# Feed-forward up and gate projections by one level of Strassen's scheme, in a Mamba-2 layer with a ternary feed-forward

## The chip, the cores and the metric

One Trainium2 chip, one core of it. The metric is the device time of one launch in microseconds (us). It is given as the median of several runs; one more execution was taken by the hardware profiler, and its trace is what the rows below come from.

## The reference, cut to what matters

There are 2 sequences of 2048 tokens with 512 features. A Mamba-2 block (input projection, short convolution, state-space scan, gate, RMS norm, output projection) is followed by residual and layer norm, then by a gated feed-forward with ternary weights and again residual and layer norm:

```python
def ternary_quant(w):
    scale = jnp.mean(jnp.abs(w)) + EPS
    q = jnp.clip(jnp.round(w / scale), -1.0, 1.0) * scale
    return w + jax.lax.stop_gradient(q - w)
wu, wg, wd = ternary_quant(W_up), ternary_quant(W_gate), ternary_quant(W_down)
# x: [tokens, 512]; W_up, W_gate: [2048, 512]; W_down: [512, 2048]
# feed-forward: (silu(x @ wg.T or x @ wu.T) * the other one) @ wd.T
```

The kernel takes the silu of the "up" product and multiplies it by the "gate" product. The 4096 tokens make NB = 8 blocks of T = 512 tokens.

## The kernel before, in words

The kernel has two stages, one after the other, each with one program for every engine; semaphores tie the programs together.

**Stage A** (to about 813 us) does the Mamba-2 block and the first layer norm, block by block. Each block has four places p = 0 to 3, and the order within a place is written out by hand for each engine. Beside it the stage makes the ternary weights: in the places of blocks 2 to 5 a piece of W_up or W_gate, in those of blocks 6 and 7 a piece of W_down. A piece is loaded (`load_quant`, line 437), its signs are taken on ACT (line 827), `quantise` on DVE (line 1205) makes -1, 0 or 1 in float16, and `store_quant` (line 442) writes it to a DRAM scratch. When the last input projection is done, the weights of up and gate are loaded over the input projection's weights (`weights`, 2 x 2 MB, line 516). The layer norm's result goes to DRAM as `x1_dram`. In each place POOL gates two heads (`yg`, line 958), and scales and subtracts for others; it waits for DVE's `y_ch` first.

**Stage B** (from about 814 us) does the feed-forward. For a block n:

- `turn(n, k)`: PE transposes the block's float32 rows into PSUM, four pieces of 128 features. ACT writes the high float16 half `x_hi` (line 1503), DVE the low half `x_lo` (line 1545).
- `up_gate(n, par, m)` for m = 0 to 15: 8 matmuls (4 pieces of the features, each with `x_hi` and `x_lo`) of 128x128 weights and 512 columns for up, 8 more for gate (line 1460). They have two PSUM banks each for up and gate.
- `hidden(n, m)`: ACT takes tanh of up (line 1508), DVE makes (tanh + 1) * up (line 1551) and multiplies by gate (line 1556), ACT makes `h_hi` (line 1512), DVE `h_lo` (line 1561).
- `down(t, par, c)` for four groups c of 128 tokens: 32 matmuls of 512 columns (line 1474) into one of two banks; then DVE's residual, statistics, POOL's power -0.5 and DVE's `normalise`, and a store.

A step t does up and gate of block t+1, and the down product of block t: after every fourth m one `turn` of block t+2 and one `down`. Ahead of step 0 the up and gate of block 0 run with no down product between them; step 7 has down products only. The queue of each engine is in this written order, and an engine whose next instruction waits holds all that is behind it. POOL has nothing in stage B but one tiny power for each group of 128 tokens.

Of the kernel before, what the change touches and what calls it, by code (L numbers as in the profile page):

```python
# [24 lines left out]
F32 = mybir.dt.float32  # L25
# [5 lines left out]
P = 128  # L31
# [9 lines left out]
KF = 16  # L41
COL_CB = 2 * H * P
# [3 lines left out]
QW = FW // NB // 2  # L46
SU = 16.0
# [95 lines left out]
def build(nc, a, out):  # L143
    with ExitStack() as ctx:
        keep = {
            "cum_dram": nc.dram_tensor("cum_dram", [2, C, H, P], F32, kind="Internal").ap(),
            "tern_dram": nc.dram_tensor("tern_dram", [3, NB, P, 2 * QW], F16, kind="Internal").ap(),
# [10 lines left out]


            "x1_out": [ctx.enter_context(nc.semaphore(f"x1_out{k}")) for k in range(2)],  # L160
            "xin_in": ctx.enter_context(nc.semaphore("xin_in")),
            "tern_in": [ctx.enter_context(nc.semaphore(f"tern_in{w}")) for w in range(3)],
# [7 lines left out]
def stage_a(nc, a, keep):  # L170
    cum_dram, tern_dram, x1_dram = keep["cum_dram"], keep["tern_dram"], keep["x1_dram"]
    weights, ident, ffn_scale, exponent = keep["weights"], keep["ident"], keep["ffn_scale"], keep["exponent"]
    passed = keep["passed"]
    with ExitStack() as ctx:
# [35 lines left out]
        quant = sb("quant", [P, 2, 2 * QW])  # L210
        raw_q = quant[:, 0, :]
        sgn = quant[:, 1, 0:QW].bitcast(F16)
        tern = quant[:, 1, QW:2 * QW].bitcast(F16)
# [5 lines left out]
        u_hi = sb("u_hi", [P, 2, KD * T], F16)  # L219
        u_lo = sb("u_lo", [P, 2, KD * T], F16)  # L220
# [11 lines left out]
        cum_b = sb("cum_b", [P, 4, C, P])  # L232
# [55 lines left out]
        tern_ok = sem("tern_ok")  # L288

# [98 lines left out]
        def _(sp):  # L388
# [11 lines left out]
            def load_abs(i):  # L400
                if i >= N_ABS:
                    return
                if i >= 2:
                    sp.wait_ge(abs_ok[i % 2], i // 2)
                sp.dma_start(quant[:, i % 2, :], a["w_ffn"][i // NB, i % NB]).then_inc(abs_in[i % 2], 16)
# [29 lines left out]
            def load_quant(n, par, p):  # L435
                w, row = quant_row(n, par, p)
                sp.dma_start(raw_q, a["w_ffn"][w, row]).then_inc(rawq_in, 16)

            def store_quant(n, par, p):
                w, row = quant_row(n, par, p)  # L440
                wait_apart(sp, tern_ok, n * 4 + (p + 1 - 4 * Q0), passed["sp"])
                sp.dma_start(tern_dram[w, row], tern).then_inc(tern_out, 16)
# [13 lines left out]
            def step(n, par):  # L456
                for p in range(4):
# [11 lines left out]
                    if is_at(n, NB):  # L469
                        if p == 1:  # L470
# [36 lines left out]
                    if quantised(n):  # L507
                        store_quant(n, par, p)
                    if p == 3 and more(n):
                        store_cum(n + 1, 1 - par, turn_use(n, "cumt"))  # L510
                        load_cum(n + 1, 1 - par, 0)
                    if p == 3 and is_at(n, NB - 1):
                        sp.wait_ge(z_full, NB * H)
                        sp.wait_ge(tern_out, 16 + 16 * NB * 2)
                        for w in range(2):
                            sp.dma_start(weights[:, w * FW:(w + 1) * FW].rearrange("p (n q) -> p n q", n=NB),
                                         tern_dram[w].rearrange("n p q -> p n q")).then_inc(keep["tern_in"][w], 16)
# [209 lines left out]
        def _(act):  # L727
# [12 lines left out]
            def magnitude(i):  # L740
                act.wait_ge(abs_in[i % 2], 16 * (i // 2 + 1))
                act.activation(quant[:, i % 2, :], quant[:, i % 2, :], ACT.Abs,
# [80 lines left out]
            def signs(n, par, p):  # L823

                w, _ = quant_row(n, par, p)
                act.wait_ge(rawq_in, n * 64 + (16 * (p + 1) - 64 * Q0))
# [88 lines left out]
        def _(pool):  # L915
# [71 lines left out]

            def step(n, par):
                for p in range(4):
# [24 lines left out]
        def _(dve):  # L1014
# [14 lines left out]
            def magnitude(i):  # L1029
                dve.wait_ge(abs_in[i % 2], 16 * (i // 2 + 1))  # L1030
                dve.tensor_reduce(abs_sum[:, i // NB, i % NB:i % NB + 1], quant[:, i % 2, :], AX.X, ALU.add,
                                  apply_absolute_value=True).then_inc(abs_ok[1], 1)
# [290 lines left out]

def stage_b(nc, keep, out):
    tern_dram, x1_dram = keep["tern_dram"], keep["x1_dram"]
    weights, ident, ffn_scale, exponent = keep["weights"], keep["ident"], keep["ffn_scale"], keep["exponent"]
    passed = keep["passed"]
    with ExitStack() as ctx:  # L1328
# [9 lines left out]
        t_ug_k = weights[:, 0:2 * FW].rearrange("p (w k e) -> p w k e", w=2, k=KD)  # L1338
# [5 lines left out]
        x_hi = sb("x_hi", [P, 2, KD, T], F16)  # L1344
        x_lo = sb("x_lo", [P, 2, KD, T], F16)
        x_res = sb("x_res", [P, 2, D])
        th = sb("ffn_th", [P, 2, T])
        act_up = sb("act_up", [P, 2, T])
        hid = sb("hid", [P, 2, T])
        h_hi = sb("h_hi", [P, 2, KF, T], F16)  # L1350
        h_lo = sb("h_lo", [P, 2, KF, T], F16)
        res = sb("ffn_res", [P, 2, D])
        stats = sb("ffn_stats", [P, 2, 6])
        mv = sb("ffn_mv", [P, 2, 2])
        var_e = sb("ffn_var_e", [P, 2])
        rstd = sb("ffn_rstd", [P, 2])
        y = sb("ffn_y", [P, 2, D])

        p_up, p_gate, p_down, p_x = ([bank(f"p_{x}{k}") for k in range(2)] for x in ("up", "gate", "down", "x"))

        tern_in, xin_in = keep["tern_in"], keep["xin_in"]
        xres_in = [sem(f"xres_in{k}") for k in range(2)]
        y_out = [sem(f"y_out{k}") for k in range(2)]
        scales_ok = sem("scales_ok")
        px_full = sem("px_full")
        xhi_ok = sem("xhi_ok")
        xlo_ok = sem("xlo_ok")
        up_full = sem("up_full")
        gate_full = sem("gate_full")
# [12 lines left out]

        def run_steps(eng, step):

            step(0, 0)
# [10 lines left out]

        def has_turn(t):

            return not (is_at(t, NB - 1) or is_at(t, NB - 2))

# [3 lines left out]
        def _(sp):  # L1404
# [258 lines left out]
```

## Time and profile before

| | us |
|---|---|
| runs | 1514.17, 1510.38, 1513.2 (median 1513.2) |
| profiled execution, whole | 1507.89 |
| its span, first to last instruction | 1506.2 |
| PE busy | 1420.2 (94%) |
| DVE busy | 958.5 (64%) |
| ACT busy | 665.1 (44%) |
| POOL busy | 354.1 (24%) |

The page's own slices of the span (40 equal ones, each digit the busy tenths of a slice):

```
PE   5787999999999999999967999999999999999998
DVE  6696787887878778787643555555555545555453
ACT  4586385673746747476441333222222223222220
POOL 0044254462534525355350000000000000000000
PEclk9798999999999999999978999999999999999999
```

The stages are seen in the POOL row: it is at work in the first half and idle in the second. PE is full in both, except at the start and where the stages meet.

### The profile page before, as it was taken

The page shows a single profiled execution, that of the slowest core. Times are in us where ns is not written, and L with a number is a line of the kernel's source. Part 1 is how long each engine was busy: PE and PEld are TensorE (multiplying, and loading weights), DVE is VectorE, ACT ScalarE, POOL GpSimd, SP SyncE. Part 2 cuts the span into 40 slices and gives each one's busy share as a digit, 9 for nine tenths or more (in the row PEclk, how much of TensorE's full clock was granted, in tenths as well). Part 3 has the DMA queues.
Part 4 walks back from the last instruction along what each step waited for, and adds up shares of the span by engine and source line. Part 5 has one row for each costly group of instructions (what it writes and reads, how often), then busy time and mean ns, then how long its engine had stood idle before and what let it go on. Part 6 is the DMA issues. An engine that isn't in the chain of part 4 may idle for free. (4 is left out here: it accounts for less than half of the span.)

```text
span 1506.2 us, 22488 instructions
## 1 busy us (share of the span) xinstructions
PE 1420.2 (94%) x7978; PEld 736.3 (49%) x7978; DVE 958.5 (64%) x1697; ACT 665.1 (44%) x1344; POOL 354.1 (24%) x392
## 2 busy tenths in 40 slices
PE   5787999999999999999967999999999999999998
PEld 2354555555655555555543444444444444444443
DVE  6696787887878778787643555555555545555453
ACT  4586385673746747476441333222222223222220
POOL 0044254462534525355350000000000000000000
PEclk9798999999999999999978999999999999999999
DMA  4735334242242522316233010100201010100101
GB/s 144 236 116 177 105 88 133 72 148 72 81 138 71 148 82 86 130 62 167 86 133 122 5 42 28 57 25 11 64 21 64 14 57 29 56 24 12 35 22 63
DMA packets 93311, 121.48 MB, mean 81 GB/s; under 512 B 6672, under 2 KB 57616, under 8 KB 91920
## 3 DMA queue, kind: packets, MB, share of 16 engines
q1 hardware_dynamic: 93200, 120.01, 25.4%
q8 instruction: 68, 1.11, 0.3%
q14 instruction: 43, 0.35, 0.1%
HBM read 96.79 MB, written 23.20 MB: 80 GB/s over the span
## 5 line engine op out<-in xcount | busy, mean ns | idle before, releaser
L574 PE MATMUL ring<-u_hi,weights 128*128 128x512 f16 x1088 | 353.9, 387 | 5.1 <-DVE x_ch L1056 5.1
L574 PE MATMUL ring<-u_lo,weights 128*128 128x512 f16 x544 | 210.3, 387 | 0.0
L1460 PE MATMUL p_up<-x_hi,weights 128*128 128x512 f16 x512 | 195.1, 381 | 3.8 <-DVE x_lo L1545 3.8
L1460 PE MATMUL p_up<-x_lo,weights 128*128 128x512 f16 x512 | 195.1, 381 | 0.0
L1460 PE MATMUL p_gate<-x_hi,weights 128*128 128x512 f16 x512 | 194.8, 381 | 0.0
L1460 PE MATMUL p_gate<-x_lo,weights 128*128 128x512 f16 x512 | 194.6, 380 | 0.0
L1474 PE MATMUL p_down<-t_down,h_hi 128*128 128x512 f16 x512 | 194.1, 379 | 0.0
L1474 PE MATMUL p_down<-t_down,h_lo 128*128 128x512 f16 x512 | 194.1, 379 | 0.0
L1512 ACT ACTIVATE h_hi<-hid 128x512 f16<-128x512 f32 x128 | 80.7, 631 | 244.1 <-DVE hid L1556 244.1
L1508 ACT ACTIVATE ffn_th<-p_up,tanh_scale 128x512 f32<-128x512 f32 x128 | 88.0, 687 | 222.6 <-PE p_up L1460 222.5
L1536 POOL TENSOR_TENSOR ffn_rstd<-ffn_var_e,exponent 128x1 f32<-128x1 f32 x32 | 17.3, 540 | 673.3 <-DVE ffn_var_e L1573 673.3
L574 PEld LDWEIGHTS ring<-u_hi,weights 128*128 128x128 f16 x1088 | 108.9, 100 | 129.6 <-issue 12.4
L601 PE MATMUL ring<-w_out,raw 128*128 128x512 f16 x768 | 169.3, 381 | 0.0
L1551 DVE SCALAR_TENSOR_TENSOR act_up<-ffn_th,p_up 128x512 f32<-128x512 f32 x128 | 88.0, 687 | 109.1 <-ACT ffn_th L1508 109.1
L1051 DVE SCALAR_TENSOR_TENSOR acc<-ring,taps,acc 128x511 f32<-128x511 f32 (+2 forms) x192 | 143.7, 748 | 4.5
L1556 DVE SCALAR_TENSOR_TENSOR hid<-act_up,hid_scale,p_gate 128x512 f32<-128x512 f32 x128 | 95.6, 747 | 48.2 <-PE p_gate L1460 47.6
L601 PEld LDWEIGHTS ring<-w_out,raw 128*128 128x128 f16 x768 | 75.6, 99 | 89.7 <-issue 1.7
L1566 DVE SCALAR_TENSOR_TENSOR ffn_res<-p_down,out_scale,x_res 128x512 f32<-128x512 f32 x32 | 24.0, 751 | 145.6 <-PE p_down L1474 145.6
L958 POOL TENSOR_TENSOR yg<-y_ch,z_ch 128x512 f32<-128x512 f32 x64 | 81.4, 1273 | 143.7 <-DVE y_ch L1171 143.7
L808 ACT ACTIVATE xdt<-p_turn,dts 128x128 f32<-128x128 f32 x256 | 72.7, 374 | 88.7 <-PE p_turn L625 88.6
L963 POOL TENSOR_TENSOR raw<-yg,raw 128x512 f16<-128x512 f32 x64 | 78.7, 1229 | 94.2 <-ACT raw L838 94.2
L1561 DVE TENSOR_TENSOR h_lo<-hid,h_hi 128x512 f16<-128x512 f32 x128 | 87.5, 684 | 0.1
(140 smaller groups left out, 2054.9 us busy)
## 6 DMA issues: line engine op xcount, KB each, us to landing
quant<-in_w_ffn SPq DMA_DIRECT2D x48, 512.0 KB, 4.4
cum_b<-cum_dram SPq DMA_DIRECT2D x64, 256.0 KB, 6.6
u_raw<-in_u_t SPq DMA_DIRECT2D x8, 1024.0 KB, 10.7
cum_g<-cum_dram SPq DMA_DIRECT2D x64, 128.0 KB, 7.2
rows<-in_u_tok SPq DMA_DIRECT2D x32, 256.0 KB, 5.9
x_dram<-rows SPq DMA_DIRECT2D x32, 256.0 KB, 2.0
u_raw<-x_dram SPq DMA_DIRECT2D x8, 1024.0 KB, 5.9
x_res<-x_dram SPq DMA_DIRECT2D x32, 256.0 KB, 2.8
```

The source lines that it names most:

```text
L574: mm = pe.matmul(ring[bank_k][:, :], w_in[:, ws, k, col:col + P], us[:, par, k * T:(k + 1) * T], start=(i == 0), stop=(i == 3 * KD - 1))
L601: mm = pe.matmul(ring[b][:, :], ys[:, h, c * P:(c + 1) * P], w_out[:, ws, h, :], start=(h == 0 and ys is y_hi and ws == 0), stop=(h == H - ...
L958: pool.tensor_tensor(yg[:, q, :], y_ch[:, q, :], z_ch[:, k % 4, :], ALU.mult).then_inc(yg_ok, 1)
L963: pool.tensor_tensor(y_lo[:, h, :], yg[:, q, :], y_hi[:, h, :], ALU.subtract).then_inc(ylo_ok, 1)
L1051: dve.scalar_tensor_tensor(acc[:, buf, k + 1:T], own[:, 0:T - 1 - k], taps[:, h, 2 - k:3 - k], acc[:, buf, k + 1:T], ALU.mult, ALU.add).th ...
L1460: mm = pe.matmul(banks[m % 2][:, :], t_ug_k[:, w, k, m * P:(m + 1) * P], xs[:, par, k, :], start=(i == 0), stop=(i == 2 * KD - 1))
L1474: mm = pe.matmul(p_down[c % 2][:, :], hs[:, par, m, c * P:(c + 1) * P], t_down[:, m, :], start=(i == 0), stop=(i == 2 * KF - 1))
L1508: act.activation(th[:, m % 2, :], p_up[m % 2][:, :], ACT.Tanh, scale=tanh_scale[:, 0:1]).then_inc(th_ok, 1)
L1512: act.activation(h_hi[:, par, m, :], hid[:, m % 2, :], ACT.Copy).then_inc(hhi_ok, 1)
L1551: dve.scalar_tensor_tensor(act_up[:, m % 2, :], th[:, m % 2, :], 1.0, p_up[m % 2][:, :], ALU.add, ALU.mult).then_inc(act_ok, 1)
L1556: dve.scalar_tensor_tensor(hid[:, m % 2, :], act_up[:, m % 2, :], hid_scale[:, 0:1], p_gate[m % 2][:, :], ALU.mult, ALU.mult).then_inc(hid ...
L1561: dve.tensor_tensor(h_lo[:, par, m, :], hid[:, m % 2, :], h_hi[:, par, m, :], ALU.subtract).then_inc(hlo_ok, 1)
```

## The change

Up and gate are computed by the Winograd form of Strassen's scheme. The weight matrix (features by outputs) and the block (features by tokens) are each cut into quarters: features 0 to 255 and 256 to 511, outputs 0 to 1023 and 1024 to 2047, tokens 0 to 255 and 256 to 511. Seven products of a quarter-sized pair take the place of eight:

- The weight factors are A11, A12, A22 and four sums S1 to S4, made of the ternary values. POOL makes the sums in stage A (`factor_sums`), four additions of 256 float16 columns for each of the 16 pieces of W_up and W_gate. Seven of eight slots of `tern_ug` are kept in SBUF: 4 in `weights`, 2 in the place of the input's split (`u_split`), 1 in that of `cum_rows`.
- The block factors are B11, B21, B22 and four sums T1 to T4. They are made in stage B: ACT copies the transposed block out of PSUM (`x_turned`), POOL makes the sums (`x_sum`, 512 float32 columns each), ACT and DVE split each of the seven into a high and a low half (`x_high`, `x_low`).
- A step has 8 pairs q in place of 16 tiles m. A pair is 128 outputs of the first half and 128 of the second, for 512 tokens. One `product` is 8 matmuls of 128x128 weights and 256 columns (up and gate share a bank). Products 1, 6 and 7 go to bank `p_x1`; 2, 4, 5 and 3 to `p_y2`, where 3 is added to 5's.
- ACT copies `p_x1` out three times (`s1`, `u2`, `u3`), DVE makes four sums c11, c12, c21, c22 of a copy and a bank; each holds up and gate of 256 tokens. Tanh, (tanh + 1) * up, the product with gate and the split then follow for each half; the product with gate moves from DVE to POOL.
- A down product is cut into four pieces of 8 matmuls, two for each pair q.
- Several double buffers become single ones (`x_res`, `ffn_res`, `y` goes, the result is stored from `ffn_res`). Up and gate of block 0 become a step -1 of the same form.

```diff
@@ build
-            "tern_dram": nc.dram_tensor("tern_dram", [3, NB, P, 2 * QW], F16, kind="Internal").ap(),
+            "tern_ug": nc.dram_tensor("tern_ug", [2, P, 8, NB, QB], F16, kind="Internal").ap(),
+            "tern_down": nc.dram_tensor("tern_down", [NB, P, 2 * QW], F16, kind="Internal").ap(),
@@ stage_a, sync: order of a place, and the loads at its end
-                    if quantised(n):
-                        store_quant(n, par, p)
                     if p == 3 and more(n):
                         store_cum(n + 1, 1 - par, turn_use(n, "cumt"))
                         load_cum(n + 1, 1 - par, 0)
+                    if quantised(n):
+                        store_quant(n, par, p)
...
+                        for k, dst, f0, nf in ((0, weights, 1, 4), (1, keep["u_split"], 5, 2)):
+                            for w in range(2):
+                                sp.dma_start(dst[:, w * nf * FS:(w + 1) * nf * FS],
@@ stage_a, gpsimd
+            def factor_sums(n, p):
+                at = n * 16 + 4 * (p - 4 * Q0)
+                wait_apart(pool, tern_ok, n * 4 + (p + 1 - 4 * Q0), passed["pool"])
+                pool.tensor_tensor(factors[:, 6, :], factors[:, 0, :], factors[:, 3, :], ALU.add).then_inc(factor_step, 1)
...
@@ stage_b, tensor
+            def product(n, par, q, j, first):
+                weight, x = FACTORS[j]
+                i = SPLIT.index(x)
+                bank_j = p_x1[q % 2] if j in (1, 6, 7) else p_y2[(3 * q + (0, 0, 2, 1, 2)[j - 1]) % 2]
...
+                for w in range(2):
+                    for k in range(2):
+                        for xs in (xs_hi, xs_lo):
+                            mm = pe.matmul(bank_j[:, w * 256:(w + 1) * 256], factor(weight, w, k, q), xs[:, par, i, k, :],
...
             def step(t, par):
...
                     if has_up(t):
+                        wait(pe, u3_ok, i - 1)
+                        product(n, own, q, 1, True)
+                        if has_down(t):
+                            down(t, par, q // 2, q % 2 * 2)
+                    if before:
+                        pe.wait_ge(c22_ok, m * NQ + (r + 1))
+                        product(m, its, r, 3, False)
+                    if has_up(t):
+                        wait(pe, c21_ok, i)
+                        product(n, own, q, 2, True)
+                        pe.wait_ge(s1_ok, i + 1)
+                        product(n, own, q, 6, False)
+                        wait(pe, c12_ok, i)
+                        product(n, own, q, 4, True)
...
+                    if has_down(t):
+                        down(t, par, q // 2, q % 2 * 2 + 1)
+                    if has_up(t):
+                        pe.wait_ge(c11_ok, i + 1)
+                        product(n, own, q, 5, True)
+                        pe.wait_ge(u2_ok, i + 1)
+                        product(n, own, q, 7, False)
+                    if has_turn(t) and q < 2:
+                        turn(t + 2, 2 * q)
+                        turn(t + 2, 2 * q + 1)
@@ stage_b, scalar: order in one pair ("before" is the pair before)
+                    if before: chain_read(m, r, u3, prod[7], u3_ok, c21_ok)
+                    if has_up(t): chain_read(n, q, s1, prod[1], s1_ok, c11_ok)
+                    if before: hidden_tanh(m, r, True); hidden_tanh(m, r, False)
+                    if has_up(t): chain_read(n, q, u2, prod[6], u2_ok, c12_ok)
+                    if before: hidden_high(m, its, r, True)
+                    if has_turn(t):
+                        if q in (1, 2): x_turned(t + 2, 2 * q - 2); x_turned(t + 2, 2 * q - 1)
+                        for j in {3: (0, 1), 4: (2, 3), 5: (4, 5), 6: (6,)}.get(q, ()): x_high(t + 2, par, j)
+                    if before: hidden_high(m, its, r, False)
@@ stage_b, gpsimd
+                    if before: hidden(m, r, True); hidden(m, r, False)
+                    if has_turn(t):
+                        for k in {3: (0,), 4: (1, 2), 5: (3,)}.get(q, ()): x_sum(t + 2, k)
+                    if has_down(t) and q % 2: norm_root(t, q // 2)
@@ stage_b, vector
+                    if before:
+                        summed(m, r, "c22", u3, u3_ok, 5, ALU.add)
+                        summed(m, r, "c21", u3, u3_ok, 4, ALU.subtract)
+                        hidden(m, r, True)
+                        summed(m, r, "c12", u2, u2_ok, 5, ALU.add)
+                    if has_up(t): summed(n, q, "c11", s1, s1_ok, 2, ALU.add)
+                    if before: hidden(m, r, False); hidden_low(m, its, r, True)
+                    if has_turn(t):
+                        for j in {3: (0, 1), 4: (2, 3), 5: (4, 5), 6: (6,)}.get(q, ()): x_low(t + 2, par, j)
+                    if has_down(t) and q % 2 == 0 and q: normalise(t, q // 2 - 1)
+                    if before: hidden_low(m, its, r, False)
+                    if has_down(t) and q % 2: residual(t, q // 2)
```

(Calls that stand on several lines in the code are put on one here.)

## Rows read from the trace of the kernel before

**Rows 1.** Stretches of the whole core: stretch, length; busy us of each engine; clock, DMA.
```profile
820.00:840.00 20.00, 20.00 (x81) 8.46 (x80) 8.23 (x12) 5.96 (x9) 0.00 (x0) 0.86 0.44 156
1000.00:1200.00 200.00, 200.00 (x948) 93.42 (x947) 102.63 (x167) 53.42 (x84) 4.86 (x9) 1.00 0.11 35
```

**Rows 2.** Chain of waits in stage B: start us, us, what.
```profile
819.79 3.59 PE p_up L1460 x8
...
826.19 1.73 PE p_up L1460 x8
...
882.08 1.90 PE p_up L1460 x8
...
896.07 0.44 PE p_x L1447 x4
896.50 6.91 PE p_down L1474 x32
```

**Rows 3.** Groups of instructions by form, stage B: count, busy us, mean ns, idle before.
```profile
L1474 PE MATMUL p_down<-t_down,h_hi 128*128 128x512 f16 x512 | 194.1, 379 | 0.0
...
L1556 DVE SCALAR_TENSOR_TENSOR hid<-act_up,hid_scale,p_gate 128x512 f32<-128x512 f32 x128 | 95.6, 747 | 48.2 <-PE p_gate L1460 47.6
L1508 ACT ACTIVATE ffn_th<-p_up,tanh_scale 128x512 f32<-128x512 f32 x128 | 88.0, 687 | 222.6 <-PE p_up L1460 222.5
...
L1561 DVE TENSOR_TENSOR h_lo<-hid,h_hi 128x512 f16<-128x512 f32 x128 | 87.5, 684 | 0.1
L1512 ACT ACTIVATE h_hi<-hid 128x512 f16<-128x512 f32 x128 | 80.7, 631 | 244.1 <-DVE hid L1556 244.1
...
L1503 ACT ACTIVATE x_hi<-p_x 128x512 f16<-128x512 f32 x28 | 16.2, 578 | 0.0
```

**Rows 4.** Groups of instructions by form, stage A.
```profile
L958 POOL TENSOR_TENSOR yg<-y_ch,z_ch 128x512 f32<-128x512 f32 x64 | 81.4, 1273 | 143.7 <-DVE y_ch L1171 143.7
...
L1149 DVE TENSOR_TENSOR seg<-p_seg,cb_mask 128x512 f32<-128x512 f32 x64 | 43.9, 686 | 20.3 <-ACT p_seg L821 20.3
...
L737 ACT ACTIVATE w_out<-rows,norm_s 128x512 f16<-128x512 f32 x8 | 5.1, 708 | 0.0
```

**Rows 5.** The instructions of line 1047: ns min/median/max, first and last start.
```profile
L1047 DVE TENSOR_TENSOR acc<-acc,corr x64: 140/660/1278, 25.6 to 758.3; 128x3 f32<-128x3 f32 x64
```

**Rows 6.** Order of time, DVE and POOL near 521 us: start us, us, instruction, [idle before].
```profile
520.86 2.37 DVE L1036 SCALAR_TENSOR_TENSOR u_lo<-u_raw,u_hi 128x2048 f16<-128x2048 f32 x1 [0.44 <-ACT u_hi L749]
...
522.19 2.05 POOL L963 TENSOR_TENSOR raw<-yg,raw 128x512 f16<-128x512 f32 x1 [1.11 <-ACT raw L838]
...
523.15 1.11 DVE L1047 TENSOR_TENSOR acc<-acc,corr 128x3 f32<-128x3 f32 x1
```

**Rows 7.** Order of time, PE near 345 us: first of 48 small matmuls and what follows.
```profile
344.97 0.24 PE L535 MATMUL p_turn<-weights,u_hi 128*128 128x8 f16 x4
...
346.18 0.38 PE L574 MATMUL ring<-u_hi,weights 128*128 128x512 f16 x1
```

**Rows 8.** Order of time, where stage B starts.
```profile
814.95 0.60 ACT L1503 ACTIVATE x_hi<-p_x 128x512 f16<-128x512 f32 x1 [34.95 <-PE p_x L1447]
```

**Rows 9.** Order of time in stage A, near 492 and 508 us.
```profile
491.75 1.28 DVE L1205 SCALAR_TENSOR_TENSOR quant<-quant,thr 128x1024 f16<-128x1024 f32 x1 [0.46 <-ACT quant L827]
...
493.91 1.27 POOL L958 TENSOR_TENSOR yg<-y_ch,z_ch 128x512 f32<-128x512 f32 x1 [4.03 <-DVE y_ch L1171]
...
508.59 1.15 ACT L827 ACTIVATE quant<-quant,thr 128x1024 f16<-128x1024 f32 x1 [1.36 <-DMA quant<-in_w_ffn]
```

**Rows 10.** Order of time, hand-overs from PE to ACT, ACT to DVE, DVE to POOL.
```profile
1453.52 0.38 PE L1460 MATMUL p_up<-x_lo,weights 128*128 128x512 f16 x1
...
1453.94 0.69 ACT L1508 ACTIVATE ffn_th<-p_up,tanh_scale 128x512 f32<-128x512 f32 x1 [7.17 <-PE p_up L1460]
1453.94 0.15 DVE L1573 TENSOR_SCALAR ffn_var_e<-ffn_mv 128x1 f32<-128x1 f32 x1
...
1454.18 0.54 POOL L1536 TENSOR_TENSOR ffn_rstd<-ffn_var_e,exponent 128x1 f32<-128x1 f32 x1 [20.18 <-DVE ffn_var_e L1573]
...
1454.66 0.69 DVE L1551 SCALAR_TENSOR_TENSOR act_up<-ffn_th,p_up 128x512 f32<-128x512 f32 x1 [0.56 <-ACT ffn_th L1508]
```

**Rows 11.** Order of time on DVE, residual to normalise of one group of tokens.
```profile
1472.93 0.75 DVE L1566 SCALAR_TENSOR_TENSOR ffn_res<-p_down,out_scale,x_res 128x512 f32<-128x512 f32 x1 [4.72 <-PE p_down L1474]
...
1474.66 0.15 DVE L1573 TENSOR_SCALAR ffn_var_e<-ffn_mv 128x1 f32<-128x1 f32 x1
1475.47 0.55 DVE L1578 TENSOR_SCALAR ffn_y<-ffn_res,ffn_mv,ffn_rstd 128x512 f32<-128x512 f32 x1 [0.66 <-POOL ffn_rstd L1536]
```

More of the change, by code:

```diff
@@ L41 @@
 KF = 16
+FS = 2048
 COL_CB = 2 * H * P
@@ L218, in stage_a @@
         u_raw = keep["u_raw"]
-        u_hi = sb("u_hi", [P, 2, KD * T], F16)
-        u_lo = sb("u_lo", [P, 2, KD * T], F16)
+        u_hi, u_lo = (keep["u_split"][:, k * 2 * KD * T:(k + 1) * 2 * KD * T].rearrange("p (b e) -> p b e", b=2) for k in range(2))
         acc = sb("acc", [P, 3, T])
@@ L1354, in stage_b @@
[L1354 to L1359, printed above, removed]
+        x_res = sb("x_res", [P, D])
+        res = sb("ffn_res", [P, D])
+        stats = sb("ffn_stats", [P, 6])
+        mv = sb("ffn_mv", [P, 2])
+        var_e = sb("ffn_var_e", [P, 1])
+        rstd = sb("ffn_rstd", [P, 1])
+        p_x1, p_y2, p_down, p_x = ([bank(f"p_{x}{k}") for k in range(2)] for x in ("chain", "prod", "down", "x"))
@@ L1383, in run_steps @@
         def run_steps(eng, step):
+            step(-1, 1)
             step(0, 0)
@@ L1476, in down @@
-                        i += 1
-                mm.then_inc(down_full, 1)
+                                       start=(e == 0 and m == 0 and hs is h_hi), stop=(m == KF - 1 and hs is h_lo),
+                                       skip_group_check=True)
+                if e == 3:
+                    mm.then_inc(down_full, 1)
             for k in range(KD):
                 turn(0, k)
-            for m in range(KF):
-                up_gate(0, 0, m)
-                if m >= KF - KD:
-                    turn(1, m - (KF - KD))
@@ new lines, in hidden_tanh, with hidden_high @@
+            def hidden_tanh(n, q, second):
+                i = n * NQ + q
+                act.wait_ge(c21_ok if second else c12_ok, i + 1)
+                act.wait_ge(c22_ok if second else c11_ok, i + 1)
+                wait(act, act_ok, 2 * i + (0 if second else 1))
+                up = c_b[:, 0, :, :] if second else c_a[:, q % 2, 0, :, :]
+                act.activation(th, up, ACT.Tanh, scale=tanh_scale[:, 0:1]).then_inc(th_ok, 1)
+            def hidden_high(n, par, q, second):
+                i = n * NQ + q
+                act.wait_ge(hid_ok, 2 * i + (1 if second else 2))
+                if q == 0 and second:
@@ L1559, in hidden_low, with x_low, summed @@
-            def hidden_low(n, par, m):
-                dve.wait_ge(hhi_ok, n * KF + (m + 1))
-                dve.tensor_tensor(h_lo[:, par, m, :], hid[:, m % 2, :], h_hi[:, par, m, :], ALU.subtract).then_inc(hlo_ok, 1)
+            def x_low(n, par, j):
+                dve.wait_ge(xhi_ok, n * 7 + (j + 1))
+                dve.tensor_tensor(xs_lo[:, par, j, :, :], place[SPLIT[j]], xs_hi[:, par, j, :, :], ALU.subtract).then_inc(xlo_ok, 1)
+            def summed(n, q, c, kept, kept_ok, j, op):
+                i = n * NQ + q
+                own = prod[3] if c == "c12" else prod[j]
+                dve.wait_ge(own, i + 1)
+                dve.wait_ge(kept_ok, i + 1)
+                half = int(c[2]) - 1
+                if c[1] == "1":
+                    dst = c_a[:, q % 2, :, half, :]
+                    wait(dve, hlo_ok, 2 * i - 2)
+                else:
+                    dst = c_b[:, :, half, :]
+                    wait(dve, hlo_ok, 2 * i - 1)
+                bank_j = p_y2[(3 * q + (0, 0, 0, 1, 2)[j - 1]) % 2]
+                dve.tensor_tensor(dst, kept.rearrange("p (w e) -> p w e", w=2),
+                                  bank_j[:, :].rearrange("p (w e) -> p w e", w=2), op).then_inc(
+                                      {"c11": c11_ok, "c12": c12_ok, "c21": c21_ok, "c22": c22_ok}[c], 1)
@@ L1581, in _ @@
+            for j in range(7):
+                x_low(0, 0, j)
             dve.tensor_scalar(tanh_scale[:, :], ffn_scale[:, 0:1], 0.5 / SX, None, ALU.mult).then_inc(scales_ok, 1)
```

385 lines of the change are left out of this document (245 added, 140 removed).

## Prediction

> **What bounds the kernel now.** I read the stretches first, then the chain of waits in stage B, the groups by form, and the order of time at single places. In stage B PE is busy for all 200 us of a stretch, at the full clock, while DVE has 103 us of work, ACT 53 and POOL 5 [rows 1]. The chain of waits is PE work throughout: eight matmuls of 512 columns in 1.73 us, 32 of them in 6.91 us, four transposes in 0.44 us [rows 2], and the down matmuls never waited [rows 3]. So PE bounds it, and the question is whether the others keep up once PE has less to do and they have more.
>
> **What PE saves.** A matmul of 512 columns takes 1.73/8 = 0.216 us. No row has 256 columns. Below: half of it, 0.108. Above: 48 matmuls of 8 columns, each with its own 128x128 weights, took 346.18 - 344.97 = 1.21 us, 0.025 each [rows 7]; were that added whole, 0.133. I take 0.109, since columns account for 512/2.4 = 213 ns of the 216 (at the full clock of 2.4 GHz) and 2.5 ns are left for each matmul. A product of 8 is then 0.875 us. A pair q costs PE 7 x 0.875 = 6.12 us; its two tiles m cost 4 x 1.73 = 6.91 before. With 3.46 of down products that is 9.58 against 10.37, 0.79 less. In steps 0 to 6 there are 56 pairs: -44.2 us if PE never waits.
>
> The Trainium skill (TensorE: Matmul & The Clock Gate, section Back-to-back issue gap) gives about 81 ns for sustained matmuls of 128 columns with their weight loads, 25 ns above its formula for the matmul alone; carried over to 256 columns the product would take 8 x 0.134 = 1.07 us and the seven more than the eight now. That rule speaks against the change; the 25 ns of the small matmuls, which include the load [rows 7], speak for hiding most of it under 107 ns of columns.
>
> **What DVE, ACT and POOL now do in a pair.** Take the moment at which PE ends product 7 of a pair as 0. Hand-overs [rows 10]: from the start of a product's last matmul to ACT 0.42 us, for 512 columns, so about 0.21 after the columns end; ACT to DVE 0.03, I use 0.05; DVE to POOL 0.09. Durations: a sum of bank and SBUF 0.69 (as `seg`), POOL's product 1.27, a copy with a scale held in SBUF 0.71 (`w_out`) [rows 4]; copy out of PSUM 0.58 to 0.60 [rows 3, 8]; tanh 0.69, low half with such a scale 0.75 (as `hid`), high half 0.63, low half without scale 0.68 [rows 3]; (tanh + 1) * up 0.69 [rows 10].
>
> u3 is read at 0.21 to 0.81, c22 starts at 0.86. From there the work is one chain through four engines, since DVE's queue is in order and each piece waits for the one before: c22 and c21 1.38, tanh 0.79 with its two hand-overs, (tanh+1)up 0.69, c12 0.69, second tanh 0.79 (c11 is hidden beside it), (tanh+1)up 0.69, POOL's product 1.36, high half 0.81, low half 0.75. That is 7.95 us from one c22 to the next. POOL's first product and the other halves lie beside it. Every second pair adds residual and statistics, 1474.81 - 1472.93 = 1.88 us [rows 11].
>
> PE's first deadline in a pair is product 3 (needs c22), the tightest is product 4: it comes after 0.875 x 4 + 1.73 = 5.23 us and needs c12, which is ready at 0.86 + 2.86 + 0.69 + 0.05 = 4.46. So DVE may be 0.77 us late; what goes beyond is a PE wait. A plain pair (7.95, with residual 9.83) fits 9.58 on average.
>
> **Pairs that also split the next block.** Pairs 3 to 6 add x_sum on POOL and x_low on DVE. Line 1047 adds two SBUF tensors of 3 columns; it takes 0.14 at best and 1.28 at worst, median 0.66, the worst being POOL's 1.27 [rows 4, 5]. At 522.19 a subtraction of POOL takes 2.05, against 1.27 for its products [rows 4], while DVE's u_lo, also with two SBUF inputs, runs to 523.23; and DVE's tiny addition of 523.15 ends at 524.26, with POOL's (524.24) [rows 6]. Whoever comes second waits for the other's whole instruction. DVE's operations with a PSUM input show nothing of it (`seg` 0.69). x_low, h_lo and (tanh+1)up have two SBUF inputs, and x_sum stands against them. Counting from c22, the low half of the second tokens starts only when POOL's product ends (6.39) and ends at 7.14. Pair 3: two x_low to 8.52, x_sum to 9.79, low half 10.54, residual 12.4. Pair 4: x_sum to 8.41, two x_low to 9.79, x_sum beside normalise to 11.11, low half 11.9. Pair 5: as pair 3, 12.4. Pair 6: one x_low and normalise, 9.1. Pair 7: 9.83 plus POOL's power 0.66 and normalise 0.55, which stands directly behind it: 11.1. Pairs 0, 1 and 2: 7.95, 10.2 and 8.45 (two x_turned of 0.58 stand ahead of the high half), against 10.46 of PE in 0 and 1, with transposes.
>
> Lateness carried over, less 9.58 for each pair: into pair 4 2.82, so PE waits 2.05 and 0.77 stays; into 5 3.09, wait 2.32; into 6 3.59, wait 2.82; into 7 0.3; into the next step's 0 1.8, wait 1.04. Sum 8.2 us for each step with a split. Six such steps (0 to 5) and 0.75 behind step 6: +50. Both ends: none at all if DVE runs ahead of my chain, and 65 if each of 56 pairs takes 0.25 more than counted. I take 50. Steps 0 to 6: -44.2 + 50 = +6.
>
> **Step -1** has no down product, so PE needs 6.12 a pair, and the chain takes over. Start: the transposes and copies end near 818.2, as before (then first matmul 819.79); product 1 starts about there. But T1, T3, T2, T4 follow each other on POOL with splits in DVE's way: 4 x 1.27 plus three x_low before the last ones gives about 828, s1 behind ACT's seven splits 828.8. Then four products at half clock (this stretch had 0.86 on average; matmuls of 3.59/8 = 0.45, half of it 0.213 at 1.2 GHz, 1.71 a product [rows 1, 2]): pair 0 ends near 835. Then c22 of pair 0 at 835.9 and seven chain rounds: 8.3 + 8.3 + 10.5 + 11.9 + 10.5 + 8.6 + 7.95 = 66.1; PE's last products end 1.75 before the next round's end, at 900.3. Before, block 1's first matmul started at 882.08: +18.2. Below, with no contention and the chain as it stands, +8; above +25.
>
> **Rest.** In step 7 product 3 waits for c22 with nothing ahead of it (1.6 us), and the last piece of the first down product for the last low half (about 1.0): +2.6; before, a down product covered that. Stage A: POOL's four sums of 256 columns, about 0.65 each from 1.27 for 512, start behind `quantise`; POOL was idle for 4.03 us before yg [rows 9], of which 0.9 are behind quantise, so gate is 1.7 late, and ACT takes it 6 us later: hidden. SP's store waits for the sums; behind it wait load_quant and the cum loads. One sign operation in four already waited 1.36 us for its load [rows 9]: 4 blocks x 0 to 2 us. The 512-byte runs and 7 MB in place of 4 at the stages' meeting land before the last layer norm. Bounds 0 and 10, I take +2. If POOL's idle time were gone, each of 16 places would cost up to 2.6 us.
>
> **Sum:** +6 + 18.2 + 2.6 + 2 = +29. On the profiled 1507.9 that is 1537; the median of the runs is 5 us above that execution, and 1538 is my figure, 1.6% above the median.
>
> **Rivals.**
> - *PE stays full (faster).* DVE and POOL do not get in each other's way where it matters: DVE's operations fall beside POOL's waits, the chain's low halves slip in. Then pairs 3 to 5 take 10.4, 9.1, 10.4; the waits are 1.2 us a step, 8 in all; steps 0 to 6 -36, step -1 +8, rest +5: -23, 1485 to 1490. For it: only some operations collide, and PE had no wait in 200 us. Against: what line 1047 and POOL's subtraction show [rows 5, 6].
> - *A draw.* Contention is there, but a third to a half less than counted, as a round starts ahead or POOL gets its turn in a gap: +22 to +30 in place of +50, +12 in step -1, +5 for the rest: -44 + 22 to 30 + 17 is -5 to +3, 1503 to 1516 with both references.
> - *Small matmuls cost their weight load* (0.134). Steps 0 to 6: 56 x (10.96 - 10.37) = +33, with few waits left (10), step -1 +20, rest +5: +68, 1576 to 1581. Against: 0.025 us for a matmul with its load [rows 7].
> - *Stage A pays*: POOL late by 2.6 us in 16 places and PE with it: +40 on any case. Against: the idle time before yg [rows 9]. Taken at 3% within the others.
>
> **How the numbers follow.** Contention as counted 0.56 (1520 to 1556), PE full 0.26 (1480 to 1505), draw 0.12, small matmuls 0.06. What a measurement can tell from no change is 0.3%, 4.5 us. Of the draw's 0.12, 0.04 goes to faster and 0.08 to same; of the first case's lower edge 0.02 goes to same: faster 0.30, same 0.10, slower 0.60. The range 1483 to 1554 leaves out the two ends.
>
> **What would show it.** Product matmuls 0.109 apart. In steps 0 to 6 PE waits for c22 or c12, mostly in pairs 4 to 6, about 8 us a step; x_low above 1.2 us where x_sum runs; step -1 near 80 us long, with PE at three quarters. I am wrong if PE is full in 1000 to 1200 us, or if the clock falls in step -1's gaps, which would add to it.

## The result, and the profile of the changed kernel

The changed kernel takes 1521.85 us (median of 5 runs, 1518.8 to 1523.78), the kernel before 1512.89 on the same chip (5 runs, 1510.38 to 1514.17): a ratio of 1.0059 [1.0042, 1.0076], 9.0 us or 0.6% slower. The two profiled executions differ by more, 1521.1 against 1506.2 us of span.

The head of its page, with the busy tenths in 40 slices:

```profile
span 1521.1 us, 27017 instructions
PE 1388.2 (91%) x9514; PEld 886.2 (58%) x9514; DVE 1119.8 (74%) x1849; ACT 812.8 (53%) x1592; POOL 609.4 (40%) x616
PE   5786999999999999999966889999989899999997
DVE  6695787887778878787644777878687867778774
POOL 0054256473655737355352333334242423333221
PEclk9898999999999999999977999999999999999999
```

Stage B begins in slice 22. PE is no longer full there, and POOL, nearly idle there before [rows 1], has work. Stretches of the same kernel (columns as in [rows 1]):

```profile
840.00:860.00 20.00, 18.26 (x164) 15.48 (x162) 15.55 (x22) 13.17 (x23) 6.36 (x5) 1.00 0.21 68
...
860.00:880.00 20.00, 15.35 (x113) 12.06 (x111) 15.15 (x21) 10.65 (x19) 9.55 (x7) 0.83 0.00 0
...
1000.00:1200.00 200.00, 190.30 (x1421) 137.91 (x1420) 153.15 (x219) 99.71 (x163) 69.02 (x58) 1.00 0.12 37
```

In 1000 to 1200 us PE idles 10 us of 200, at the full clock; DVE went from 103 us to 153 and is not full either. The waits behind 800 us (engine, line, waited for: total us, times, longest):

```profile
PE p_prod L1551 <- DVE c_b L1757: 39.0, 28, 3.3
...
PE p_chain L1551 <- DVE xs_lo L1741: 8.2, 2, 6.1
```

So PE waits mostly for c22, the sum that must have read the bank to which product 3 is then added: a chain of hand-overs, not an engine at its limit. PE in order of time:

```profile
833.52 0.37 PE L1551 MATMUL p_chain<-xs_hi,weights 128*128 128x256 f16 x1 [6.12 <-DVE xs_lo L1741]
...
1109.35 0.28 PE L1551 MATMUL p_prod<-xs_hi,cum_rows 128*128 128x256 f16 x1 [1.13 <-DVE c_b L1757]
1109.46 0.27 PE L1551 MATMUL p_prod<-xs_lo,cum_rows 128*128 128x256 f16 x1
...
1235.55 0.28 PE L1551 MATMUL p_chain<-xs_hi,weights 128*128 128x256 f16 x1 [2.04 <-ACT rows L1641]
...
1236.81 0.63 PE L1566 MATMUL p_down<-t_down,h_lo 128*128 128x512 f16 x1
1237.24 0.63 PE L1566 MATMUL p_down<-t_down,h_hi 128*128 128x512 f16 x1
```

Matmuls of 256 columns start 0.11 us apart, each with new weights. The row at 1235.55 stands where the hardware loop goes from its first round to its second, and comes 2.3 us after the last matmul of the first round (1233.23). The down matmuls behind it start 0.43 us apart in place of 0.22: the granted clock of 1236 to 1240 us is 0.57, partly at 1.2 GHz.

A round is the time from one c22 to the next (the first of the two `c_b` sums). DVE in pairs 3 and 4 of step 2, which runs inside the hardware loop, then POOL's sum in the same place:

```profile
1101.19 0.69 DVE L1765 SCALAR_TENSOR_TENSOR c_a<-rows,c_a 128x512 f32<-128x512 f32 x1
1102.55 1.24 DVE L1772 SCALAR_TENSOR_TENSOR h_lo<-c_b,hid_scale,h_hi 128x512 f16<-128x512 f32 x1 [0.66 <-ACT h_hi L1658]
1103.71 1.28 DVE L1741 TENSOR_TENSOR xs_lo<-x_f,xs_hi 128x512 f16<-128x512 f32 x2
1104.92 1.75 DVE L1772 SCALAR_TENSOR_TENSOR h_lo<-c_a,hid_scale,h_hi 128x512 f16<-128x512 f32 x1
...
1108.21 0.18 DVE L1785 BATCH_NORM_AGGREGATE ffn_mv<-ffn_stats 128x2 f32<-128x6 f32 x1 [0.15 <-DVE ffn_stats L1783]
...
1108.60 1.28 DVE L1757 TENSOR_TENSOR c_b<-rows,p_prod 128x512 f32<-128x512 f32 x2
1110.76 0.69 DVE L1765 SCALAR_TENSOR_TENSOR c_b<-rows,c_b 128x512 f32<-128x512 f32 x1 [0.87 <-ACT rows L1650]
...
1119.84 1.27 DVE L1757 TENSOR_TENSOR c_b<-rows,p_prod 128x512 f32<-128x512 f32 x2
```
```profile
1104.47 1.65 POOL L1713 TENSOR_TENSOR x_f<-x_f 128x512 f32<-128x512 f32 x1 [1.23 <-DVE xs_lo L1741]
```

The same pair 3 in step 1, ahead of the loop, with POOL's product and sum; then the two c22 behind it:

```profile
1013.66 1.28 DVE L1757 TENSOR_TENSOR c_b<-rows,p_prod 128x512 f32<-128x512 f32 x2 [1.46 <-ACT rows L1641]
...
1018.70 1.27 POOL L1703 TENSOR_TENSOR c_a<-c_a 128x512 f32<-128x512 f32 x1 [0.91 <-DVE c_a L1765]
...
1019.43 1.08 DVE L1772 SCALAR_TENSOR_TENSOR h_lo<-c_b,hid_scale,h_hi 128x512 f16<-128x512 f32 x1 [0.82 <-ACT h_hi L1658]
1020.44 1.28 DVE L1741 TENSOR_TENSOR xs_lo<-x_f,xs_hi 128x512 f16<-128x512 f32 x2
1021.26 1.59 POOL L1713 TENSOR_TENSOR x_f<-x_f 128x512 f32<-128x512 f32 x1 [1.29 <-DVE xs_lo L1741]
1021.64 1.75 DVE L1772 SCALAR_TENSOR_TENSOR h_lo<-c_a,hid_scale,h_hi 128x512 f16<-128x512 f32 x1
...
1025.14 1.28 DVE L1757 TENSOR_TENSOR c_b<-rows,p_prod 128x512 f32<-128x512 f32 x2
...
1036.22 1.27 DVE L1757 TENSOR_TENSOR c_b<-rows,p_prod 128x512 f32<-128x512 f32 x2
```

The low half at 1104.92 takes 1.75 us, a microsecond more than [rows 3] have for it, beside POOL's sum. And two sums at once take 1.28 us: back to back, DVE's operations start 0.60 to 0.64 us apart though each record is 0.68 or 0.69 long. Groups by form behind 815 us (columns as in [rows 3]):

```profile
L1772 DVE SCALAR_TENSOR_TENSOR h_lo<-c_b,hid_scale,h_hi 128x512 f16<-128x512 f32 x64 | 85.1, 1329 | 37.5 <-ACT h_hi L1658 37.4
...
L1772 DVE SCALAR_TENSOR_TENSOR h_lo<-c_a,hid_scale,h_hi 128x512 f16<-128x512 f32 x64 | 60.8, 951 | 7.8 <-ACT h_hi L1658 7.8
...
L1741 DVE TENSOR_TENSOR xs_lo<-x_f,xs_hi 128x512 f16<-128x512 f32 x56 | 53.9, 995 | 6.7 <-ACT xs_hi L1635 6.7
...
L1713 POOL TENSOR_TENSOR x_f<-x_f 128x512 f32<-128x512 f32 x32 | 51.5, 1610 | 26.3 <-DVE xs_lo L1741 26.2
```

**Where the 15 us of the two profiles went**, from the starts of PE's matmuls:

| | before | after | difference | predicted |
|---|---|---|---|---|
| start of stage B | 813.82 | 818.36 | +4.5 | +2 |
| step -1, to the first matmul of step 0 | 68.3 | 80.9 | +12.7 | +18.2 |
| steps 0 to 6 | 590.65 | 583.0 | -7.6 | +6 |
| step 7, to the last down matmul | 27.6 | 33.0 | +5.4 | +2.6 |

### The profile page after: what moved, and what is told of

Read it like the earlier page. It is cut to its first block and busy times, and to the rows that moved or that the text cites. A ratio compares the mean times of both kernels' runs of the same rounds, so it can differ in the third digit from the quotient of the medians.

```text
span 1521.1 us, 27017 instructions
## 1 busy us (share of the span) xinstructions
PE 1388.2 (91%) x9514; PEld 886.2 (58%) x9514; DVE 1119.8 (74%) x1849; ACT 812.8 (53%) x1592; POOL 609.4 (40%) x616
## 5 line engine op out<-in xcount | busy, mean ns | idle before, releaser
L607 PE MATMUL ring<-u_split,weights 128*128 128x512 f16 x1632 | 388.7, 389 | 5.3 <-DVE x_ch L1103 5.3
L607 PEld LDWEIGHTS ring<-u_split,weights 128*128 128x128 f16 x1632 | 158.9, 101 | 183.2 <-issue 20.0
L1703 POOL TENSOR_TENSOR c_b<-c_b 128x512 f32<-128x512 f32 x64 | 81.6, 1275 | 259.8 <-DVE c_b L1765 259.8
L1641 ACT ACTIVATE rows<-p_chain 128x512 f32<-128x512 f32 x192 | 113.6, 594 | 121.4 <-PE p_chain L1551 118.9
L1551 PE MATMUL p_chain<-xs_hi,weights 128*128 128x256 f16 x512 | 120.9, 276 | 10.2 <-DVE xs_lo L1741 8.2
L1551 PE MATMUL p_prod<-xs_hi,weights 128*128 128x256 f16 x512 | 121.8, 277 | 0.2
L1551 PE MATMUL p_prod<-xs_lo,weights 128*128 128x256 f16 x512 | 121.2, 276 | 0.0
L1551 PE MATMUL p_chain<-xs_lo,weights 128*128 128x256 f16 x512 | 121.0, 276 | 0.0
L1772 DVE SCALAR_TENSOR_TENSOR h_lo<-c_b,hid_scale,h_hi 128x512 f16<-128x512 f32 x64 | 85.1, 1329 | 37.5 <-ACT h_hi L1658 37.4
L1757 DVE TENSOR_TENSOR c_b<-rows,p_prod 128x512 f32<-128x512 f32 x128 | 82.0, 682 | 31.4 <-ACT rows L1641 23.0
```

The source lines that it names most:

```text
L607: mm = pe.matmul(ring[bank_k][:, :], w_in[:, ws, k, col:col + P], us[:, par, k * T:(k + 1) * T], start=(i == 0), stop=(i == 3 * KD - 1))
L1551: mm = pe.matmul(bank_j[:, w * 256:(w + 1) * 256], factor(weight, w, k, q), xs[:, par, i, k, :], start=(first and w == 0 and k == 0 and xs ...
L1641: act.activation(dst, p_x1[q % 2][:, :], ACT.Copy).then_inc(ok, 1)
L1703: pool.tensor_tensor(gate, up, gate, ALU.mult).then_inc(hid_ok, 1)
L1757: dve.tensor_tensor(dst, kept.rearrange("p (w e) -> p w e", w=2), bank_j[:, :].rearrange("p (w e) -> p w e", w=2), op).then_inc({"c11": c1 ...
L1772: dve.scalar_tensor_tensor(h_lo[:, par, m, :].rearrange("p (h e) -> p h e", h=2), hid, hid_scale[:, 0:1], h_hi[:, par, m, :].rearrange("p ...
```

## The experiments

Ratios are to the kernel before on the same chip, with their 95% intervals. "Step" is the time from one step's first down matmul to the next one's, 84.63 us in the kernel before; in the changed kernel 82.67, 83.03, 84.04, 86.53, 85.27, 84.31 and (into step 7) 80.36. The experiments ran on three chips; the kernel before took 1513.2, 1511.8 and 1515.3 us there, so ratios compare better than times.

**1. Contention: POOL's sums cut to one element.**

```
-                pool.tensor_tensor(place[a], place[b], place[c], ALU.subtract)...
+                pool.tensor_tensor(place[a][:, 0:1, 0:1], place[b][:, 0:1, 0:1], place[c][:, 0:1, 0:1], ALU.subtract)...
```

> The changed kernel with POOL's four sums of the block (x_sum) on one element in place of 512 columns; the waits and all other work stay, so T1 to T4 are not computed. Theory (POOL's sums and DVE's two-SBUF operations exclude each other, and that makes PE's waits in pairs 4 to 6): the low halves there fall from 1.75 and 2.35/2 to 0.75 and 0.64 us, the rounds of pairs 3, 4, 5 from 11.7, 11.2, 11.8 to 10.7, 9.2, 10.7 us, the waits from 5.3 to about 1.2 us a step: 25 us in six steps and 4 in step -1, so 1493 us. Rival (it is the mere length of the chain with the added splits): waits stay above 4 us a step and the time within 8 us of 1522.

Measured: 1489.56 us, ratio 0.9841 [0.9828, 0.9854], 3.4 us below what I expected. T1 to T4 are not made here, so it is good for timing only. Its groups by form:

```profile
L1772 DVE SCALAR_TENSOR_TENSOR h_lo<-c_a,hid_scale,h_hi 128x512 f16<-128x512 f32 x64 | 47.7, 745 | 7.8 <-ACT h_hi L1658 7.7
L1741 DVE TENSOR_TENSOR xs_lo<-x_f,xs_hi 128x512 f16<-128x512 f32 x56 | 36.1, 680 | 6.9 <-ACT xs_hi L1635 6.9
```

With no sum to stand against, this low half is back at 745 ns and x_low at 680; the other low half (h_lo<-c_b), which stands against POOL's product, stays at 1331. The first steps fall to 78.5 and 78.9 us and step -1 (to the first down matmul) from 81.8 to 71.8. POOL's four sums a block cost the changed kernel some 32 us in all: their own time in the chain and the time they take from DVE together, which this run does not part.

**2. The sums moved to DVE**, each behind the x_low it needs (the lines taken out are POOL's, those put in DVE's; block 0's sums move in the same way).

```
-                        for k in {3: (0,), 4: (1, 2), 5: (3,)}.get(q, ()):
-                            x_sum(t + 2, k)
+                        for j, k in {3: ((0, None), (1, 0)), 4: ((2, 1), (3, 2)), 5: ((4, 3), (5, None)), 6: ((6, None),)}.get(q, ()):
                             x_low(t + 2, par, j)
+                            if k is not None:
+                                x_sum(t + 2, k)
```

> The four sums of the block move from POOL to DVE, 0.61 to 0.69 us each, all computed. Theory of exclusion: DVE gets 2.6 us a step more but loses 4.1 us of standing still; rounds of 11.4, 10.5, 11.3, waits 3.8 in place of 5.3 us a step: 9 us less, 1513, and step -1 starts its second half earlier. Rival (DVE is simply the full engine there): 2.6 us more of waits a step, 1535 or more.

Measured: 1507.52 us, 0.9968 [0.9955, 0.9981]. A sum takes 683 ns on DVE against 1610 on POOL, and PE in 1000 to 1200 us goes from 190.3 to 193.4 us. This version is just faster than the kernel before, and 5.5 us below what I expected. Step -1 (to the first down matmul) stays near where it was, 80.8 for 81.8, and its seven rounds take 61.3 us for 61.2: as I read it, the sums' place in DVE's queue costs there what the contention did.

**3. The gate product moved to DVE.**

```
                         hidden(m, r, True)
+                        gated(m, r, True)
...
                         hidden(m, r, False)
+                        gated(m, r, False)
```

(`gated` is POOL's product, `tensor_tensor(gate, up, gate, ALU.mult)`, in DVE's program; POOL's is taken out.)

> The product with gate goes back from POOL to DVE (two operations of 0.61 to 0.69 us a pair), POOL keeps the block's sums. Theory (a round is a chain of four engines, POOL's 1.36 us one link of it): the round of a plain pair stays near 7.5, as 1.36 + 0.5 us of standing still go and 1.3 come; contention with x_sum stays; 0 to 10 us less, 1512 to 1522. Rival (DVE's busy share decides: 76% now, 90% then): 10 to 30 us more.

Measured: 1521.51 us, 1.0049 [1.0034, 1.0064], the changed kernel again, and at the upper end of what I expected. The other low half (h_lo<-c_b) falls from 1329 to 746 ns, POOL's product of 1.27 us is gone from the chain, and its 0.69 us now stands in DVE's queue, which works 162 us of 200. PE's waits only change their name (20.7 us of them are now for the c_a sums, 22.5 for c_b).

**4. The halves of the first tokens one pair later**, out of the chain from c22 to c22.

```
+        def pair_two(t, par, q):
+            if q > 1:
+                return (t + 1, 1 - par, q - 2) if has_up(t) else None
+            return (t, par, NQ - 2 + q) if has_down(t) else None
...
                         summed(m, r, "c21", u3, u3_ok, 4, ALU.subtract)
+                    late = pair_two(t, par, q)
+                    if late:
+                        hidden_low(*late, False)
...
-                    if before:
-                        hidden_low(m, its, r, False)
```

and the same on ACT for the high half.

> High and low half of the first tokens are made one pair later, behind s1 on ACT and behind c21 on DVE, where DVE stands idle 0.87 us for tanh. Theory (the chain through four engines sets the rounds): the round loses POOL's product, high and low half of the first tokens (2.9 us) and keeps the second low half behind POOL's product, so 7.0 in place of 7.6, and x_sum no longer stands ahead of the first low half: waits 2 in place of 5.3 us a step, step -1 8 us shorter, about 1497 us. Rival (DVE's work and the exclusion alone count, the order doesn't): within 5 us of 1522.

Measured: 1488.15 us, 0.9829 [0.9813, 0.9845], 9 us better than expected. DVE in order of time:

```profile
1104.29 1.27 DVE L1764 TENSOR_TENSOR c_b<-rows,p_prod 128x512 f32<-128x512 f32 x2
1105.48 0.74 DVE L1779 SCALAR_TENSOR_TENSOR h_lo<-c_a,hid_scale,h_hi 128x512 f16<-128x512 f32 x1
1106.43 0.69 DVE L1772 SCALAR_TENSOR_TENSOR c_b<-rows,c_b 128x512 f32<-128x512 f32 x1 [0.21 <-ACT rows L1656]
...
1109.68 1.49 DVE L1779 SCALAR_TENSOR_TENSOR h_lo<-c_b,hid_scale,h_hi 128x512 f16<-128x512 f32 x1 [0.40 <-ACT h_hi L1664]
1111.10 2.35 DVE L1748 TENSOR_TENSOR xs_lo<-x_f,xs_hi 128x512 f16<-128x512 f32 x2
```

The low half now stands in the 0.87 us in which DVE waits for the tanh, where POOL runs no sum, and takes 0.74. So the edit does two things at once: it takes a link out of the round, and it takes this low half out of the sum's way. Its mean falls from 951 to 750 ns: the 13 that took 1.75 us in the changed kernel, all in pairs 3 and 4, are gone, 13 us of DVE's time in a gain of 34. The run does not part the two further. In step -1 the seven rounds go from 61.2 to 55.7 us. The rest of the contention has not gone: x_low (mean 1014 ns), the other low half (1299) and POOL's sum (1614) are as slow as in the changed kernel. A round is now short enough to bear them: the first two steps take 78.69 us each, and PE works 197.9 us of 200 in 1000 to 1200 us.

**5. The kernel before once more**, one execution, for the start of stage B.

> The kernel before once more, for a second profile: where in stage A the changed kernel's 4.5 us lie. If they are the change's, the first output projection starts again near 154 us and stage B near 814; if they are scatter between executions, this one lies nearer to the changed kernel's 157 and 818.

Measured: stage B starts at 817.56 us (813.82 in the first profile, 818.36 in the changed kernel). From the first output projection to that start it is 661.88 us here, 659.76 in the first profile, 660.49 in the changed kernel, and 659.2 to 663.5 over the others. Two executions of the same kernel lie 3.7 us apart, so most of the table's +4.5 can be scatter. Over the ten profiles of kernels with the change stage B starts at 814.33 to 820.19 us, 817.7 on average, against 815.7 for the two before: neither the +2 that was counted nor zero is excluded.

**6. Step 7: the down piece ahead of product 3.**

```
+                    elif has_down(t):
+                        down(t, par, q // 2, q % 2 * 2)
                     if before:
...
-                    elif has_down(t):
-                        down(t, par, q // 2, q % 2 * 2)
```

> The changed kernel with one edit of order on PE in step 7: the first piece of the down product stands ahead of product 3, which waits for c22. Theory: the wait of 2.7 us goes, and with it the 1.7 us that eight matmuls at 1.2 GHz lose behind it: 3 to 4.5 us less, 1518. Rival (the wait comes back at the last low half, and the clock falls by itself): under 1 us.

Measured: 1523.85 us, 1.0074 [1.006, 1.0087]: nothing gained, as the rival had it. PE near the end:

```profile
1485.44 0.28 PE L1551 MATMUL p_prod<-xs_hi,cum_rows 128*128 128x256 f16 x1 [0.93 <-DVE c_b L1757]
...
1492.48 0.39 PE L1566 MATMUL p_down<-t_down,h_hi 128*128 128x512 f16 x1 [2.54 <-DVE h_lo L1772]
```

PE's idle time before product 3 shrinks from 2.66 to 0.93 us, and 2.54 come back before the matmuls that need the last low half: the end is set by the chain from the last c22.

**7. Numbers 4, 2 and 6 together.**

> Late low half, the block's sums on DVE and the order of step 7 together. With the late low half alone a step already took 78.7 us, and 78.4 is PE without any wait, so the sums bring little there; step -1 and step 7 remain: 1483 (1480 to 1487). Rival (the sums on DVE bring their 14 us again): 1475 or less.

Measured: 1492.65 us, 0.9855 [0.9833, 0.9877]; missed by 10, and no better than number 4 alone. Where PE is full already, taking the sums off POOL can give nothing, and on DVE they lengthen the steps (79.11 us in place of 78.69): the two gains were ways around one chain and do not add.

**8. Number 7 with the gate product on DVE.**

> The same and the product with gate on DVE as well, so that POOL has only the power left. The round of step -1 becomes 6.6 in place of 7.0 us, PE needs 6.1: 3 us less than the one before, 1480. Rival (DVE at over 85% of a pair stands in PE's way in steps 0 to 6, where residual and splits come on top): waits come back in pairs 3 to 5, 1490 or more.

Measured: 1502.8 us, 0.9943 [0.993, 0.9957]. That is 23 us above what I expected, and 10 us worse than number 7, as the rival had it. The contention is gone (both low halves take 0.75 us, x_low 0.68), but DVE works 168.6 us of 200, PE waits 17.4 us for the c_a sums and 9.0 for c_b, and steps are 80.4 to 84.2 us.

**9. The loop over the middle steps written out** (the changed kernel, and then number 4).

```
-                with eng.Fori(0, (NB - 4) // 2) as i:
+                for i in range((NB - 4) // 2):
```

> The changed kernel with stage B's loop of two rounds of two steps written out, the work and its order unchanged. In the changed kernel the steps inside the loop took 84.0 to 86.5 us, the ones ahead of it 82.7 and 83.0, and at the loop's jump PE stood 2.2 us and then ran at 1.2 GHz. Theory (the loop costs this: counts held in registers lengthen the hand-overs of the chain, and PE's longer program is not there at the jump): steps 2 to 5 become 83.0 us like step 1, about 8 us less, 1513.5. Rival (these steps differ by something else, code loading would come anyway): within 3 us of 1522, or more than it.

> The late low half with the loop written out as well. There the steps ahead of the loop took 78.7 us and those in it 79.6 to 81.3. Theory of the loop: all at 78.7, 5.5 us less, 1483. Rival: PE is full in these steps anyway, under 2 us.

Measured: 1514.25 us, 0.9993 [0.9984, 1.0001] (12 runs), and 1484.61 us, 0.9792 [0.9779, 0.9804], 0.8 and 1.6 us above what I expected. Written out, the changed kernel has steps of 82.65, 83.02, 83.01, 83.03, 83.02 and 83.02 us, and no gap where the jump was; together the steps of the changed kernel take 8.4 us more. DVE of the unrolled kernel in a middle step:

```profile
1109.15 0.18 DVE L1785 BATCH_NORM_AGGREGATE ffn_mv<-ffn_stats 128x2 f32<-128x6 f32 x1
...
1111.55 0.69 DVE L1765 SCALAR_TENSOR_TENSOR c_b<-rows,c_b 128x512 f32<-128x512 f32 x1 [0.79 <-ACT rows L1650]
```

In the loop the same two stand behind idle times of 0.15 and 0.87 us (the rows of the changed kernel at 1108.21 and 1110.76): these hand-overs are 0.12 and 0.08 us longer there. The rounds part the cost. Eight rounds from one c22 to the next take 83.0 us written out and 84.3 in the loop, away from the jump: 1.3 us a step, 5.2 in four steps. The round with the jump takes 13.78 us in place of 10.94, and the next one 9.26 for 8.92: 3.2 more. Together that is the 8.4. At the jump PE stands 2.3 us, and DVE stands too, with nothing that the trace shows to wait for (u3 had been copied out at 1234.56):

```profile
1238.55 1.28 DVE L1757 TENSOR_TENSOR c_b<-rows,p_prod 128x512 f32<-128x512 f32 x2 [2.76 <-issue]
```

The kernel before has the same loop, its steps are 84.63 us in the loop and out of it, and PE stands nowhere near its jump. Why was not tested. That PE was full there does not explain it alone: in number 4 PE works 197.9 us of 200 and still stands 1.5 us at the jump, and the steps 0 to 6 of number 4 take 6.6 us more than written out. With both changes every step but the last takes 78.69 us and PE works 199.5 us of 200: that is PE's bound with seven products, but for one wait of 0.18 us a step. It is the fastest version here, 2.1% below the kernel before.

## Why the prediction was right in direction and 16 us too high

The figure on record was 1538. By its own terms, +29 on the median of 1513.2, it should have been 1542; 4 us came off it without a term.

- **PE's saving** held. Products of 0.875 us were counted, and their matmuls start 0.109 us apart. The full step takes 78.69 against 84.63, so 7 x 5.94 = 41.6 us are saved where 44.2 were counted; the rest is mostly the one short wait a step that number 9 still has. The rival of a weight load that is not hidden is excluded (0.11 us between starts).
- **The mechanism** held: sums on POOL lengthen DVE's chain in pairs 3 to 5, and PE waits for c22 behind them. Number 1 gives back 32 us when they are taken away; number 4 gives back 34 with the sums still on POOL, by taking one low half out of the round and out of their way. One of the signs that were named did not come: 8 us of waits a step were, 4.4 came.
- **The step that failed is "Counting from c22 ... Pair 3 ... 12.4, Pair 4 ... 11.9, Pair 5 ... 12.4", summed to +50 us of waits.** Ahead of the loop, and in every step of number 8, these rounds take 11.48, 11.08 and 11.42 us (11.73, 11.24 and 11.76 in the loop), so each was counted 0.8 to 1.0 us too long. The cause is that I strung the operations together by the length of their records. Pair 3 of step 1 against the prediction, link by link: up to the end of POOL's product 6.31 us (6.39 counted). From there each record overlaps the one ahead of it: the low half ends 0.54 us behind the product (0.75 counted), two x_low 1.21 later (1.38), x_sum 1.13 later (1.27), the second low half 0.54 later (0.75), and the next c22 starts 1.75 later (1.88). So DVE behind DVE saves 0.05 to 0.09 us an operation, and DVE behind POOL 0.2: who comes second is held until the other ends, as was told, but then needs less than its whole record. In the steps ahead of the loop PE waits 0.95, 1.43, 1.81 and 0.22 us (from one matmul's start to the next, less the usual 0.11) where 2.05, 2.32, 2.82 and 1.04 were counted: 4.4 a step, some 26 us in steps 0 to 6 in place of 50. That is the size given to the draw.
- **What the draw left out** is the loop, +8.4 us, which no step of the prediction has: -41.6 + 26 + 8.4 = -7.2, measured -7.6. Without it (number 9) the changed kernel is the draw, 0.9993. That the time still lies in the likeliest case's own range, at its foot (1520), is luck: it has the contention of another case and a cost that none had.
- **Step -1**: +12.7 for +18.2. PE's first product starts at 824.18; product 6, the third, waits 6.1 us for the sums and their splits and starts at 833.52. The first c22 comes 21.3 us after stage B's start (22.1 counted), and the seven rounds behind it take 61.2 us where 66.1 were counted, as I take it for the same reason as above. The worry over the clock there came true in part: it was 0.83 in 860 to 880 us, where PE had gaps.
- **Step 7**: +5.4 for +2.6. Product 3 comes 2.8 us late in place of 1.6; the clock falls behind that wait (0.72 in 1484 to 1490 us, down matmuls 0.43 apart), 1.7 us that I had not counted; product 3's own 0.9 us stands in this step and had been left out; the 1.0 for the last low half did not come. Number 6 shows that the order of PE's work there is not the cause.
- **Stage A**: +2 was counted, and scatter of 3.7 us hides it (number 5). The sum of my terms from the profile was +29; the profiles differ by 14.9, of which up to 4 can be this scatter, and the medians by 9.

What stays open: why the jump costs PE and DVE what it does here and nothing in the kernel before, and whether it is wait counts held in registers that lengthen the hand-overs inside the loop; writing the loop out takes away both. And step -1 at 77.4 us in the best version, where 71.8 is possible with the sums gone (number 1), was not tried further.

## What to carry to other kernels

Taking work off a full engine is worth what the chain behind it leaves. So first draw one round of that chain with every hand-over, and look for a link that can be done a round later, best where it also meets no slow neighbour; here that one edit turned +0.6% into -1.7%. When a chain is added up, take the distance between the starts of back-to-back instructions, and from the end of what held one up to its own end, not the length of the records. A hardware loop whose cost did not show before (84.63 us in it and out of it) can show after the change (8.4 us): write it out once and see.

## What the runs showed of the hardware beyond what was expected

- DVE's operations of 512 columns overlap by 0.05 to 0.09 us back to back: a record is 0.69 us, two take 1.28.
- A low half on DVE (two SBUF tensors) and a sum of POOL's on SBUF tensors hold each other up both ways: the low half takes 0.75 us alone and 1.75 beside the sum; POOL's sum takes 1.26 at its shortest and 1.61 on average. The low half that stood behind POOL's product ended 0.54 us after it. DVE's 256 sums of an SBUF and a PSUM tensor take 0.67 to 0.69 us each, whatever POOL does.
- The second round of a hardware loop began with 2.3 us in which PE did nothing and 2.8 in which DVE did nothing, and matmuls at 1.2 GHz followed: 3.2 us in all, and 1.3 us more for each of the four steps inside it.
- 256-column matmuls with new 128x128 weights each start 0.109 us apart.
